# Graph network on one core: TensorE raises its semaphores once per group instead of once per product

## Chip, cores and metric

One core of one Trainium2 chip. The metric is the device time of one execution in microseconds. Three executions of the kernel before gave 2978.41, 2980.54 and 2985.08 us; their median is 2980.54 us.

## The reference, cut to what matters

3125 nodes of 256 features, 53125 edges (50000 both ways and 3125 self loops, sorted by dst). Four layers, each `x = layernorm(x + layer(x))`:

```python
def layer0(x):                      # applied twice with a relu between
    agg = segment_sum(x[src], dst) / maximum(count, 1)
    return agg @ Wl.T + bl + x @ Wr.T          # 256 -> 512 -> 256
def layer1(x):                      # three hops
    Hn = segment_sum(H[cols] * edge_weight, rows) @ Wn.T + bn
    H = elu(Hn + H @ Ws.T + bs)                # no elu after the last
def layer2(x):                      # interaction, out and in degrees in the scale
    msg = ((x @ W1)[src] + x[src] * x[dst] @ W2) / scale
    return normalize(leaky_relu(x @ W1 + segment_sum(msg, dst) + b))
def layer3(x):                      # attention, 8 heads of 32
    h = x @ W;  e = leaky_relu(a_src[src] + a_dst[dst])
    p = exp(e - segment_max(e, dst)[dst])
    out = segment_sum(h[src] * p, dst) / segment_sum(p, dst) + bias
    return layernorm(out)
```

Sums over edges in the first three layers are matrix products: a matrix of edge counts (or weights) between nodes is built once and multiplied with the node rows. The last layer gathers rows by edge and sums them with one-hot products.

## The kernel before, in words

A class `Program` holds one queue of instructions per engine. `op` (L125 and on) appends a function that first waits for its tokens (semaphore, count), then issues one instruction that raises that engine's own "done" semaphore by one, and returns the token of the new count. `T` (L315) is `op` for TensorE. Every engine runs its queue in order. Nodes are 25 tiles of 128 (`NODE_TILES`). Edges without self loops are 416 tiles of 128 (`EDGE_TILES`), four of which are a quad (`GROUP`).

**Stages in order of time.** About 40 to 300 us: the count matrix is built. VectorE makes windows of one-hots (L540), TensorE multiplies them (`build_pe`, L545 to L560), ACT (ScalarE) keeps finished windows (`build_act`, L562 to L581). TensorE and ACT load step numbers into registers and wait on semaphores against them.

332 to 530 us, first pass over the count matrix (`first_tile`, L1080), 530 to 739 us the dense layers (`to_hidden` L1197 and `from_hidden` L1212, products of four matmuls each, each matmul an `op`), 739 to 930 us the second pass (`multiply_tile`, L954 to L975). In a pass each of 24 further node tiles is the sum of 25 products in five groups of five. ACT widens the counts of a group from 16 to 32 bits into one buffer, `count_columns` (`widen_group`, L936): the cast of group g for the next tile waits until TensorE has used group g for this tile, which it learns from `s_a_used`, raised after each group. Beside these stages GpSimd scatters the edge weights into a dense matrix by indirect transfers (L794), paced by `multiplied_beside` (L827 to L838), which waits for given counts of TensorE's semaphores; VectorE forms the sums that go there (L849).

949 to 1990 us, three hops (`hops_pe`, L1457 and on; L1526 are the products with the dense weight matrix, which come from memory through a ring).

1990 to 2280 us, third pass and layer 2. 2280 to 2545 us, the expansion: 112 stages (`expansion_pe`, L2209 and on). In a stage VectorE builds one-hots (L2298), TensorE makes six products (`by_high`, L2226) that raise `s_first`, VectorE masks the result (`mask_rows`, L2311), and TensorE adds the masked rows up (`pick`, L2237), raising `s_picked`. Sixteen stages are a cut. GpSimd gathers rows by edge meanwhile (L2134), at the pace of the masks.

2565 to 2903 us, the merge: 440 steps in 110 quads. Rows of a quad lie in one of 16 places. For nine places of 16 they were gathered during the expansion, kept in memory, and are loaded by SyncE (`load_rows`, L2180); for seven of 16, so quads 96, 98, 100 and 102 at the end, GpSimd gathers them directly (L2134, four transfers each). Both wait in `place_free` (L2137) until the place is free: 4(quad - 16) + 28 steps done, so nine quads of steps before their own number. There are 104 quads of rows and, since a tile whose edges end at two node tiles takes two steps, 110 of steps. Between its quads GpSimd has one other piece, `gather_last` (L2453, 25 indirect transfers). VectorE scales the rows of quad q + 1 (`scale_rows`, L2486) and builds the one-hots of quad q (`node_hots`, L2492), which lie in two halves in turn, so that they wait for quad q - 2 to be multiplied. TensorE (`merge_pe`, L2531) loads 20 step registers at a time, waits for the one-hots once per quad, and adds each step's product to the bank of its node tile. A step is one instruction and shows as two matmul records. ACT (`merge_act`, L2536 and on) takes each node tile's sum when the step that ends it is done and starts that bank anew.

The semaphore of the merge is `s_mm`, raised once a step. Its readers are `place_free`, `node_hots` and `merge_act`:

```python
e.wait_ge(s_mm, mm0 + (quad - PLACES) * GROUP + GROUP - 1 + NODE_TILES)      # place_free
e.wait_ge(s_mm, quad * GROUP + (mm0 - GROUP))                                 # node_hots
e.wait_ge(s_mm, e.snap(ends_of_node[d], min_val=1, max_val=MERGE_STEPS + UNROLL))   # merge_act
```

The functions that the change touches, and what calls them:

## Time and profile before

| | us |
|---|---|
| median of the runs | 2980.54 (2978.41 to 2985.08) |
| span of the profiled execution | 2974.2 |
| TensorE busy | 2470.6 (83%) |
| VectorE busy | 1396.0 (47%) |
| ScalarE busy | 707.2 (24%) |
| GpSimd busy | 936.7 (31%) |
| mean granted TensorE clock | 0.920 |

The profiled execution has no device time of its own beside its span: the first to the last recorded instruction is 2974.2 us, and the median of the runs is 6.3 us above it.

How to read the table and the rows. PE is TensorE, PEld its weight loads, DVE VectorE, ACT ScalarE, POOL GpSimd, SP SyncE; L2531 is line 2531. A group of the page is: line, engine, operation, what it writes and reads, how often | busy us, mean ns of one | idle us of the engine just before it, and what ended most of that. A row of the timeline is: start, duration, engine, line, operation, how many in a row, and in brackets the idle time before with its releaser. "remote" and "another core or an unknown queue" stand for a semaphore event whose author the profile could not find, "issue" for time in which nothing shown was waited for. Matmuls are pipelined, so their single durations overlap.

### The profile page before, as it was taken

What the parts mean: (1) busy time and instruction counts of PE and PEld (TensorE: products, weight loads), DVE (VectorE), ACT (ScalarE), POOL (GpSimd) and SP (SyncE); (2) the same over time, 40 slices, a digit from 0 to 9 for tenths busy, and PEclk for the clock granted to TensorE, in tenths of its full rate; (3) what the DMA queues carried; (4) which work ended last, traced back from release to release, by engine and by line L of the source; (5) the groups of instructions that cost most, each with busy time, mean ns of one, the idle gap of its engine ahead of it and who ended that gap; (6) DMA issues with size and microseconds to landing.
All of it is one profiled execution on the core that took longest, in us unless ns stands there. A gap on an engine that the chain in (4) does not pass through costs nothing. (4 is left out here: it accounts for less than half of the span.)

```text
span 2974.2 us, 32381 instructions
## 1 busy us (share of the span) xinstructions
PE 2470.6 (83%) x9483; PEld 1621.2 (55%) x9484; DVE 1396.0 (47%) x3940; ACT 707.2 (24%) x1552; POOL 936.7 (31%) x927
## 2 busy tenths in 40 slices
PE   3677789897987999999999999999977886457680
PEld 2444788343766555565556555577743444345560
DVE  7999656455665001030101001455575664546668
ACT  3776545111443000010001000255400000103112
POOL 0000256666666000000000000012167666576740
PEclk9888999998998999999999999999988998678885
DMA  6565678343344743444444434333558887646641
GB/s 233 243 253 225 212 238 264 118 138 97 112 121 137 152 151 129 151 134 151 129 152 133 151 119 145 93 106 102 113 168 271 278 282 245 209 132 190 192 127 43
DMA packets 209534, 493.89 MB, mean 166 GB/s; under 512 B 46457, under 2 KB 128430, under 8 KB 209134
## 3 DMA queue, kind: packets, MB, share of 16 engines
q1 hardware_dynamic: 135185, 301.30, 32.2%
q10 hardware_dynamic: 38173, 133.27, 12.8%
q0 software_dynamic: 36032, 57.60, 7.1%
q8 instruction: 67, 1.10, 0.1%
q14 instruction: 77, 0.63, 0.1%
HBM read 374.71 MB, written 117.32 MB: 165 GB/s over the span
## 5 line engine op out<-in xcount | busy, mean ns | idle before, releaser
L794 POOL DMA_INDIRECT table_dense_weights<-pair_weight,dst x416 | 411.2, 988 | 563.5 <-DVE weights_c L849 324.8
L1526 PE MATMUL banks<-own_term,features_and_rows 128*128 128x391 f32 (+1 forms) x1656 | 552.3, 491 | 0.0
L2134 POOL DMA_INDIRECT features_and_rows<-table_heads,src x376 | 401.7, 1068 | 191.4 <-issue 107.9
L1526 PEld LDWEIGHTS banks<-own_term,features_and_rows 128*128 128x128 f32 x1656 | 312.2, 189 | 226.8
L1552 DVE TENSOR_SCALAR features_and_rows<-banks,hop_bias 128x391 f32<-128x391 f32 (+1 forms) x24 | 15.0, 625 | 762.2 <-PE banks L1526 762.2
L954 PE MATMUL banks<-split_rows,count_columns 128*128 128x512 f32 x1200 | 322.1, 415 | 19.6 <-issue 12.6
L2531 PE MATMUL banks<-features_and_rows,edge_to_window 128*128 x880 | 233.4, 427 | 104.5 <-DVE edge_to_window L2492 71.6
L1526 PE MATMUL banks<-features_and_rows 128*128 128x391 f32 (+1 forms) x840 | 282.4, 491 | 0.0
L954 PEld LDWEIGHTS banks<-split_rows,count_columns 128*128 128x128 f32 x1200 | 226.3, 193 | 76.8 <-issue 21.7
L2531 PEld LDWEIGHTS banks<-features_and_rows,edge_to_window 128*128 128x128 f32 x880 | 181.3, 210 | 156.5 <-issue 122.5
L558 PE MATMUL banks<-features_and_rows,pair_and_bias_rows 128*128 128x400 f16 x806 | 184.3, 388 | 87.1 <-DVE features_and_rows L540 51.9
L936 ACT CAST count_columns<-hidden 128x640 fp32r<-128x640 f16 x310 | 212.4, 723 | 157.2 <-PE banks L954 62.2
L1526 PEld LDWEIGHTS banks<-features_and_rows 128*128 128x128 f32 x840 | 158.4, 189 | 114.6
L2004 POOL DMA_INDIRECT ble_values_at_first_edge<-dst,row_of_first_edge x50 | 48.0, 961 | 516.9 <-DVE ln_rstd L1983 464.9
L1601 POOL DMA_INDIRECT features_and_rows<-table_hop,node_of_tail_row x6 | 5.7, 953 | 638.1 <-DMA table_hop<-tmp 637.1
L558 PEld LDWEIGHTS banks<-features_and_rows,pair_and_bias_rows 128*128 128x128 f16 x806 | 110.8, 152 | 160.9 <-issue 147.6
L540 DVE TENSOR_SCALAR features_and_rows<-counter_fp,features_and_rows 128x400 f16<-128x400 f16 x806 | 198.4, 335 | 0.0
L2226 PE MATMUL banks<-features_and_rows,pair_weight 128*104 128x512 bf16 (+1 forms) x672 | 169.8, 393 | 29.9 <-DVE features_and_rows L2298 19.1
L1543 ACT ACTIVATE features_and_rows<-banks,hop_bias 128x391 f32<-128x391 f32 (+1 forms) x24 | 14.1, 587 | 728.1 <-PE banks L1526 728.1
L1080 PE MATMUL banks<-split_rows,count_columns 128*128 128x258 f32 (+1 forms) x1200 | 158.6, 291 | 13.4 <-issue 10.2
L2237 PE MATMUL banks<-edge_to_window,edge_weight 104*128 104x512 f32 (+1 forms) x224 | 123.1, 634 | 53.2 <-DVE edge_to_window L2311 32.1
L2226 PEld LDWEIGHTS banks<-features_and_rows,pair_weight 128*104 128x104 bf16 x672 | 89.8, 137 | 131.9 <-issue 75.4
(425 smaller groups left out, 3016.8 us busy)
## 6 DMA issues: line engine op xcount, KB each, us to landing
hidden<-table_counts SPq DMA_DIRECT2D x305, 160.0 KB
table_dense_weights<-weights_c ACTq DMA_DIRECT2D x26, 1600.0 KB, 5.7
own_term<-table_dense_weights SPq DMA_DIRECT2D x52, 782.0 KB
features_and_rows<-table_rows_by_edge SPq DMA_DIRECT2D x58, 528.0 KB
own_term<-table_dense_weights SPq DMA_DIRECT2D x34, 780.5 KB
pair_and_bias_rows<-table_edge_rows ACTq DMA_DIRECT2D x50, 512.0 KB
weights_c<-table_edge_rows ACTq DMA_DIRECT2D x50, 512.0 KB
table_rows_by_edge<-features_and_rows SPq DMA_DIRECT2D x48, 528.0 KB
```

What stands on the lines that cost most here:

```text
L540: made = e.tensor_scalar(hot_ring[:, s % HOTS, q, :], counter[:, 0:WIDE], steps_key[:, q, s:s + 1], None, ALU.is_equal)
L558: m = e.matmul(banks[:, bass.ds(bank_at, WIDE)], low_ring[:, s // LOWS_AT_ONCE % LOW_BLOCKS, :, 2 * (s % LOWS_AT_ONCE) + q], hot_ring[:, s ...
L794: e.indirect_dma_start(out=self.table, out_offset=bass.IndirectOffsetOnAxis(ap=self.place[:, t:t + 1], axis=0), in_=self.values[:, t:t + 1 ...
L936: e.copy(in_group(count_columns, g), in_group(slot_of(q), g)).then_inc(s_a_wide, 1)
L954: m = e.matmul(to[:, 0:2 * DIM], lhs_of(k), both_pieces(k), start=(k == first), stop=False, skip_group_check=True)
L1080: m = e.matmul(to(wide), count_columns[:, k, :], piece(k, h, wide), start=(k == 0 and h == 0), stop=False, skip_group_check=True)
L1526: m = e.matmul(psum[b][:, 0:wide], z_block(block)[:, f * P:(f + 1) * P], streamed[tile % STREAM][:, lo - from_column:lo - from_column + wi ...
L2004: e.indirect_dma_start(out=t_start[c], out_offset=bass.IndirectOffsetOnAxis(ap=start_at[:, j:j + 1], axis=0), in_=node_pair[:, j, c * HEAD ...
L2134: e.indirect_dma_start(out=to[:, k, :], out_offset=None, in_=t_h, in_offset=bass.IndirectOffsetOnAxis(ap=src[:, t:t + 1], axis=0)).then_in ...
L2226: m = e.matmul(psum[i % 2][head_rows, 0:n], table[:, q, c, :], low_hot[i % 2][c][:, 0:n], start=(c == 0 and q == 0), stop=(c == 1 and q == ...
L2237: e.matmul(psum[2 + b % 2][:, 0:n], sum_heads[head_rows, at:at + P], masked[i % 2][head_rows, 0:n], start=(r == 0), stop=(r == SCAN_ROWS - ...
L2531: e.matmul(banks[:, bass.ds(column_at, ATT_ROW)], onehot[:, k % UNROLL, :], wide_rows[:, bass.ds(row_at, ATT_ROW)], start=False, stop=Fals ...
```

## The change

Where one product or one group of transposes takes several matmuls, only the last raises a semaphore (`last=`; the others are queued by `part`). `s_a_used` is raised after the third and the fifth group of a tile in the first two passes. `s_mm` is raised on the fourth step of a quad. `s_picked` is raised once per cut, and the wait for it in `mask_rows` is dropped. All waits are rewritten in the new counts. Waits against a register go through `wait_loaded`, which writes the loaded value ANDed with 511 into a second register and waits on that, in place of a register move. Instructions and their order are otherwise the same.

```diff
+        def part(self, e, fn, *waits):
...

+        def wait_loaded(e, sem, loaded, bound):
+            e.reg_alu(bound, loaded, 511, ALU.bitwise_and)
+            e.wait_ge(sem, bound)
-        T = lambda fn, *w: pr.op("pe", fn, *w)
+        T = lambda fn, *w, last=True: pr.op("pe", fn, *w) if last else pr.part("pe", fn, *w)
...
-                e.wait_ge(s_a_used, min(45 + 4 * (half_step - IN_ROWS) + 2 * half, of_group(Q1, 0) + NODE_TILES * COUNT_GROUPS - 1))
+                e.wait_ge(s_a_used, min(2 * (45 + 4 * (half_step - IN_ROWS) + 2 * half) // 5, used(Q2 - 1, COUNT_GROUPS - 1)))
-                e.wait_ge(pr.done["pe"], dense_layers_from[0] + max(1, 6 * (half_step - IN_LAYERS) - 10 + 3 * half))
+                e.wait_ge(pr.done["pe"], dense_layers_from[0] + max(1, (6 * (half_step - IN_LAYERS) - 10 + 3 * half) // 4))
...
+        USED_AT = (COUNT_GROUPS // 2, COUNT_GROUPS - 1)
+        used = lambda q, g: q * len(USED_AT) + (1 if g <= USED_AT[0] else 2) if q < Q3 else of_group(q - Q3, g) + Q3 * len(USED_AT)
-                    e.wait_ge(s_a_used, of_group(q - 1, g))
+                    e.wait_ge(s_a_used, used(q - 1, g))
-                    m.then_inc(s_a_used, 1)
+                    if g in USED_AT:
+                        m.then_inc(s_a_used, 1)
...
                     m = T(lambda e, q=q, l=l, r=r, ps=ps, wdt=wdt: e.matmul(ps[:, 0:wdt], l, r, start=(q == 0), stop=(q == 3)),
-                          freed if q == 0 else None, scaled[c], xt_ready if q == 0 else None, l_w)
+                          freed if q == 0 else None, scaled[c], xt_ready if q == 0 else None, l_w, last=q == len(pairs) - 1)
-                          freed if mt == 0 else None, made[c])
+                          freed if mt == 0 else None, made[c], last=mt == K_HID - 1)
...
-        V(lambda e: e.tensor_scalar(merge_control[0:1, MERGE_STEPS:], ends_at, float(UNROLL), None, ALU.add), (s_merge, 1))
+        ends_known = V(lambda e: e.tensor_scalar(merge_control[0:1, MERGE_STEPS:], ends_at, float(UNROLL * GROUP + GROUP - 1), None, ALU.add), (s_merge, 1))
+        V(lambda e: e.tensor_scalar(merge_control[0:1, MERGE_STEPS:], merge_control[0:1, MERGE_STEPS:], 2, None, ALU.arith_shift_right),
+          ends_known)
...
-                e.wait_ge(s_mm, mm0 + (quad - PLACES) * GROUP + GROUP - 1 + NODE_TILES)
+                e.wait_ge(s_mm, mm0 + (quad - PLACES) + (GROUP - 1 + NODE_TILES) // GROUP)
...
-                e.matmul(psum[2 + b % 2][:, 0:n], ...).then_inc(s_picked, 1)
+                m = e.matmul(psum[2 + b % 2][:, 0:n], ...)
+                if r == SCAN_ROWS - 1:
+                    m.then_inc(s_picked, 1)
...
-                if i >= 2:
-                    e.wait_ge(s_picked, i - 1)
...
-                e.wait_ge(s_picked, SCAN_ROWS * (b + 1))
+                e.wait_ge(s_picked, b + 1)
...
-                e.wait_ge(s_mm, quad * GROUP + (mm0 - GROUP))
+                e.wait_ge(s_mm, quad + (mm0 - 1))
...
-                    e.wait_ge(s_begun, step % 32)
-                    e.matmul(banks[:, bass.ds(column_at, ATT_ROW)], onehot[:, k % UNROLL, :], wide_rows[:, bass.ds(row_at, ATT_ROW)],
-                             start=False, stop=False, skip_group_check=True).then_inc(s_mm, 1)
+                    e.wait_ge(s_begun, step & 31)
+                    m = e.matmul(banks[:, bass.ds(column_at, ATT_ROW)], onehot[:, k % UNROLL, :], wide_rows[:, bass.ds(row_at, ATT_ROW)],
+                                 start=False, stop=False, skip_group_check=True)
+                    if k % GROUP == GROUP - 1:
+                        m.then_inc(s_mm, 1)
...
-                e.wait_ge(s_mm, e.snap(ends_of_node[d], min_val=1, max_val=MERGE_STEPS + UNROLL))
+                wait_loaded(e, s_mm, ends_of_node[d], bound)
```

The groups of transposes, the running sum over nodes, the two build functions and the wait of the weight stream are changed in the same two ways.

## Rows read from the trace of the kernel before

**Rows 1.** The page's groups (columns: "How to read the table" above).

```profile
L1526 PE MATMUL banks<-own_term,features_and_rows 128*128 128x391 f32 (+1 forms) x1656 | 552.3, 491 | 0.0
...
L2531 PE MATMUL banks<-features_and_rows,edge_to_window 128*128 x880 | 233.4, 427 | 104.5 <-DVE edge_to_window L2492 71.6
...
L936 ACT CAST count_columns<-hidden 128x640 fp32r<-128x640 f16 x310 | 212.4, 723 | 157.2 <-PE banks L954 62.2
...
L540 DVE TENSOR_SCALAR features_and_rows<-counter_fp,features_and_rows 128x400 f16<-128x400 f16 x806 | 198.4, 335 | 0.0
```

**Rows 2.** Busy table by stretch: each engine's busy us (instructions), PEclk, DMA share, GB/s.

```profile
739.00:930.00 191.00, 166.89 (x675) 129.70 (x675) 133.75 (x175) 84.73 (x131) 126.61 (x132) 0.94 0.39 112
2290.00:2545.00 255.00, 190.95 (x692) 102.16 (x692) 144.84 (x283) 1.49 (x2) 165.64 (x168) 0.87 0.81 263
2640.00:2902.00 262.00, 197.88 (x784) 155.83 (x783) 169.95 (x191) 53.63 (x225) 162.89 (x148) 0.90 0.56 174
```

**Rows 3.** Chain of waits in 2540:2974, shares by line.

```profile
by line: PE banks L2531 37.1%; another core or an unknown queue 14.3%; issue 13.6%; DVE features_and_rows L2486 8.1%; DVE edge_to_window L2492 4.1%; DVE ln_stats L759 3.9%; DVE features_and_rows L2409 2.3%; DVE features_and_rows L2592 2.3%;
```

**Rows 4.** Timeline 2584:2642 of TensorE, VectorE, GpSimd (start, us, work, idle before).

```profile
2587.35 3.39 PE L2531 MATMUL banks<-features_and_rows,edge_to_window 128*128 x8 [4.26 <-DVE edge_to_window L2492]
2597.20 3.88 PE L2531 MATMUL banks<-features_and_rows,edge_to_window 128*128 x8 [6.46 <-DVE edge_to_window L2492]
...
2610.23 0.69 DVE L2492 TENSOR_TENSOR edge_to_window<-banks,dst_of_step 128x512 f32<-128x512 f32 x1 [12.20 <-issue]
...
2628.43 0.69 DVE L2492 TENSOR_TENSOR edge_to_window<-banks,dst_of_step 128x512 f32<-128x512 f32 x1 [16.35 <-remote]
...
2611.63 0.94 POOL L2453 DMA_INDIRECT tmp<-table_running_max,row_of_last_edge  x1 [0.30 <-issue]
```

**Rows 5.** Timeline 2716:2742 (TensorE, VectorE), and VectorE's wait in 2640:2902.

```profile
2715.73 2.39 PE L2531 MATMUL banks<-features_and_rows,edge_to_window 128*128 x10
...
2728.86 0.69 DVE L2492 TENSOR_TENSOR edge_to_window<-banks,dst_of_step 128x512 f32<-128x512 f32 x1 [7.36 <-remote]
...
DVE edge_to_window L2492 <- remote: 43.9, 7, 7.4
```

**Rows 6.** Timeline of TensorE, 2840:2852.

```profile
2840.45 9.16 PE L2531 MATMUL banks<-features_and_rows,edge_to_window 128*128 x40 [0.65 <-issue]
2850.67 1.59 PE L2531 MATMUL banks<-features_and_rows,edge_to_window 128*128 x6 [1.07 <-DVE edge_to_window L2492]
```

**Rows 7.** GpSimd: wait and group in 2540:2905, last transfer; TensorE's end.

```profile
POOL features_and_rows L2134 <- remote: 7.6, 4, 3.4
...
L2134 POOL DMA_INDIRECT features_and_rows<-table_heads,src x184 | 203.9, 1108 | 98.9 <-issue 47.2 <-PE banks L2531 28.9 <-DMA table_running_max<-features_and_rows 9.2
...
2871.97 0.95 POOL L2134 DMA_INDIRECT features_and_rows<-table_heads,src  x1 [0.30 <-issue]
...
2875.72 17.55 PE L2531 MATMUL banks<-features_and_rows,edge_to_window 128*128 x64 [6.46 <-DVE edge_to_window L2492]
2893.82 9.16 PE L2531 MATMUL banks<-features_and_rows,edge_to_window 128*128 x40 [0.55 <-issue]
```

**Rows 8.** Waits in the expansion, 2290:2545 (us in total, times, longest).

```profile
PE banks L2237 <- DVE edge_to_window L2311: 31.7, 10, 9.4
...
DVE edge_to_window L2311 <- remote: 30.1, 6, 6.3
```

**Rows 9.** Waits in 530:739 (first row) and 739:930.

```profile
PE banks L1197 <- issue: 15.2, 13, 2.5
...
ACT count_columns L936 <- PE banks L954: 55.6, 31, 5.7
...
PE banks L954 <- ACT count_columns L936: 6.9, 5, 2.7
```

**Rows 10.** Timeline of TensorE, 504:512.

```profile
507.85 0.28 PE L1080 MATMUL banks<-split_rows,count_columns 128*128 128x256 f32 x1 [0.43 <-issue]
```

**Rows 11.** Timeline of TensorE in the hops.

```profile
999.70 21.24 PE L1526 MATMUL banks<-own_term,features_and_rows 128*128 128x391 f32 x64
```

More of the change, by code:

```diff
@@ L142, in op, with emit @@
         return sem, self.count[sem.name]
+    def part(self, e, fn, *waits):
+        waits = [w for w in waits if w is not None]
+        def emit(eng):
+            for s, v in waits:
+                eng.wait_ge(s, v)
+            fn(eng)
+        self.queue[e].append(emit)
     def dma(self, e, sem, out, in_, *waits):
@@ L565, in build_act @@
             regs = [e.alloc_register(f"window_end_{k}") for k in range(ROTATING)]
+            bound = e.alloc_register("window_end_step")
             for b in [RUN_BANK, RUN_BANK + 1, *range(ROTATING)]:
@@ L639, in residual_gnn @@
                 m = T(lambda e, i=i, values=values, lo=lo, n=n: e.transpose(psum[i][0:n, lo:lo + P], values[:, lo:lo + n], ident[:, :]),
-                      keyed, c_id, counts_kept)
+                      keyed, c_id, counts_kept, last=lo == lasts[-1][0])
             at_row = turned_rows[:, r * 512:(r + 1) * 512]
@@ L733, in late_prep @@
                     m = T(lambda e, i=i, values=values, lo=lo, n=n: e.transpose(psum[i][0:n, lo:lo + P], values[:, lo:lo + n],
-                                                                                ident[:, :]), prepared["halves"], found)
+                                                                                ident[:, :]), prepared["halves"], found,
+                          last=lo == lasts[-1][0])
                 A(lambda e, i=i, r=r: e.copy(index_row[:, r, 0:3 * P], psum[i][:, 0:3 * P]), m)
@@ L1009, in run @@
                 m = multiply_rows(e, psum[0], lambda k: count_columns[:, k, :], (k,), 0, True)
-                if k % COUNT_GROUP == COUNT_GROUP - 1:
+                if k % COUNT_GROUP == COUNT_GROUP - 1 and k // COUNT_GROUP in USED_AT:
                     m.then_inc(s_a_used, 1)
@@ L1035, in residual_gnn @@
                 next(steps)
-        multiplied_tail = (s_a_used, of_group(Q1, COUNT_GROUPS - 1))
+        multiplied_tail = (s_a_used, used(Q1, COUNT_GROUPS - 1))
         tail_split = split(K_FOLD, psum[0][:, 0:DIM], multiplied_tail)
@@ L1081, in first_tile @@
                                      skip_group_check=True)
-                m.then_inc(s_a_used, 1)
+                if g in USED_AT:
+                    m.then_inc(s_a_used, 1)
             first_folded(e, n, to, False)
@@ L1167, in running_sum @@
             before = lambda n: ps[:, n * 32:n * 32 + NODE_TILES]
-            T(lambda e: e.matmul(before(0), triangle, counts, start=True, stop=True), freed, tri)
+            T(lambda e: e.matmul(before(0), triangle, counts, start=True, stop=True), freed, tri, last=False)
             m = T(lambda e: e.matmul(before(1), ones[:, :], counts, start=True, stop=True))
@@ L1268, in residual_gnn @@
         widen(Q2 + 1)
-        split(K_FOLD, psum[0][:, 0:DIM], (s_a_used, of_group(Q2, COUNT_GROUPS - 1)))
+        split(K_FOLD, psum[0][:, 0:DIM], (s_a_used, used(Q2, COUNT_GROUPS - 1)))
         folded2 = [build_fold(1, s_row2)]
@@ L1299, in turn0 @@
                     m = T(lambda e, ps=ps, j=j, k=k: e.transpose(ps[:, k * P:(k + 1) * P], x[:, j, k * P:(k + 1) * P], ident[:, :]),
-                          freed, t)
+                          freed, t, last=k == K_IN - 1)
                 reader[i] = A(lambda e, ps=ps, j=j: e.copy(xT[:, :, j * P:(j + 1) * P],
@@ L1628, in hops_sp @@
                         e.load([reg], steps_needed[0:1, tile:tile + 1])
-                        e.wait_ge(weights.steps, e.snap(reg, min_val=1, max_val=STEPS))
+                        wait_loaded(e, weights.steps, reg, stream_register[1])
                     elif tile == BODY * 4:
@@ L1762, in residual_gnn @@
                 m = T(lambda e, ps=ps, j=j, k=k: e.transpose(ps[:, k * P:(k + 1) * P], xT[:, k, j * P:(j + 1) * P], ident[:, :]),
-                      freed, *hops_done)
+                      freed, *hops_done, last=k == K_IN - 1)
             turned_late[j] = i, ps, m
@@ L1816, in residual_gnn @@
         widen(Q3 + 1)
-        tail_ready3 = split(K_FOLD, psum[0][:, 0:DIM], (s_a_used, of_group(Q3, COUNT_GROUPS - 1)))
+        tail_ready3 = split(K_FOLD, psum[0][:, 0:DIM], (s_a_used, used(Q3, COUNT_GROUPS - 1)))
         low_value = src_lo_hot[:, :, :].rearrange("p k n -> p (k n)").rearrange("p (c n) -> p c n", c=2)
@@ L2061, in first_rows @@
             e.wait_ge(*prepared["index"])
-            e.wait_ge(s_a_used, of_group(Q3 + NODE_TILES - 1, COUNT_GROUPS - 1))
+            e.wait_ge(s_a_used, used(Q3 + NODE_TILES - 1, COUNT_GROUPS - 1))
             for k in range(ROWS_KEPT // 2):
@@ L2236, in pick @@
                 at = P - HEADS - r * HEADS
-                e.matmul(psum[2 + b % 2][:, 0:n], sum_heads[head_rows, at:at + P], masked[i % 2][head_rows, 0:n],
-                         start=(r == 0), stop=(r == SCAN_ROWS - 1)).then_inc(s_picked, 1)
+                m = e.matmul(psum[2 + b % 2][:, 0:n], sum_heads[head_rows, at:at + P], masked[i % 2][head_rows, 0:n],
+                             start=(r == 0), stop=(r == SCAN_ROWS - 1))
+                if r == SCAN_ROWS - 1:
+                    m.then_inc(s_picked, 1)
             def turn_held(b):
@@ L2397, in residual_gnn @@
         T(lambda e: e.matmul(psum[6][:, 0:P], back[:, 0:1].broadcast_to([P, P]), ident[:, :], start=True, stop=True),
-          spread_max, masks_ok)
+          spread_max, masks_ok, last=False)
         m = T(lambda e: e.matmul(psum[6][:, P:2 * P], back[:, last:].broadcast_to([P, P]), ident[:, :], start=True, stop=True))
```

19 lines of the change are left out of this document (10 added, 9 removed).

## The prediction

> **What bounds the kernel now.** I first took the granted clock and the busy table by stretch, then the chain that ended last, then the timeline of the places where that chain is not TensorE. No single engine bounds the whole run. In the hops TensorE does: its largest group shows idle 0.0 before 1656 matmuls [rows 1]. In the build VectorE does, with idle 0.0 before its 806 comparisons [rows 1]. The merge is different. In 2640 to 2902 us TensorE is busy 197.9 of 262 us, VectorE 170.0, GpSimd 162.9 [rows 2]: nobody is full. The group of its matmuls (L2531) shows 104.5 us idle, 71.6 of them before a release by VectorE's one-hots (L2492) [rows 1]. And the chain of the last 434 us is TensorE's matmuls for only 37.1%, while 14.3% is "another core or an unknown queue" and 13.6% "issue" [rows 3]. There is one core, so an unknown releaser is a semaphore event that the profile could not pair with work in time.
>
> The timeline says what it is. The one-hots of a quad (four steps, two matmul records each) may be built once the quad two before is multiplied. TensorE multiplied one quad from 2587.35 on for 3.39 us, so until 2590.74, and the next from 2597.20 to 2601.08 [rows 4]. The one-hots that need the first of them start at 2610.23, 19.5 us after it ended, VectorE having sat idle 12.20 us; those that need the second start at 2628.43, 27.4 us after, with 16.35 us idle [rows 4]. GpSimd meanwhile issues one indirect transfer after another, 0.94 us long and 0.30 apart [rows 4]. It recurs later: the quad until 2718.12 is answered at 2728.86, VectorE idle 7.36 us [rows 5]. In a calm place the same loop makes 40 matmuls, five quads, in 9.16 us [rows 6]. So in such spells TensorE has multiplied, and its count reaches VectorE 10 to 27 us late. I read it so: every step raises the semaphore by one, VectorE needs the fourth raise of a quad, and while GpSimd issues transfers the raises are delivered slowly, one behind the other: 14 to 18 us between one-hots are 3.5 to 4.5 us a raise, 9.2 us at 2720 are 2.3. The number of raises is what the change divides by four. In 2640 to 2902 alone VectorE idles 43.9 us before L2492 on the unknown releaser [rows 5].
>
> **Part 1, the merge.** 440 raises become 110, and every condition stands at the same step as before, since both sides counted in quads already; only the node sums' ends are rounded up, by at most three steps, 3 x 2 x 0.229 = 1.4 us [rows 6]. ACT waits there for a sum of a bank reused several tiles later, so I cost it at nothing; if that cover is gone it is 1.4 us at the last tile. One tiny VectorE operation is added in the hops, where TensorE shows no idle: 0.
>
> What goes, if the delay goes: of the chain's 434 us, 62 us unknown and 59 us issue [rows 3]. Issue contains the loads of step registers, 22 of them, 10.22 us from block start to block start less 9.16 [rows 6], so 1.07 us x 22 = 23 us, which stay. Up to about 98 us are then at stake. But GpSimd is late next. Its queue is nearly continuous: in 2540 to 2905 it idles only 28.9 us for TensorE and 7.6 us for unknown releasers beside its fixed 0.30 us per transfer [rows 7]. Its last transfer starts at 2871.97 [rows 7]. With those 36.5 us gone it starts at 2835.5. It belongs to quad 102 of 110; eight quads remain, at the 64 matmuls in 17.55 us of the end [rows 7], plus one transfer and one scaling (0.95 + 1.25) and some landing, say 3 us: 2835.5 + 3 + 17.5 = 2856. TensorE's last block ends at 2893.82 + 9.16 = 2903.0 [rows 7]. The gain with GpSimd as the floor is 47 us. I take **42**, since one raise per quad can still be late: at 2.3 to 4.5 us each it can exceed the 2.04 us (10.22 / 5) that a quad takes. Bounds: 3 (a raise costs only its own time, below) and 76 (the 184 transfers average 1.108 us against an undisturbed 0.95, so 29 us more could go [rows 7]).
>
> **Part 2, the expansion.** 112 raises of `s_picked` become 7, and the mask's wait on it goes; TensorE's order implied it. There VectorE's masks (L2311) idle 30.1 us on unknown releasers and TensorE's picks (L2237) wait 31.7 us for masks [rows 8], while GpSimd is busy 165.6 of 255 us with 168 instructions [rows 2], 216 us with 0.30 each. `s_first`, the raise that the mask really needs, stays at one per stage, so the raises are halved only. Of 31.7 us I take a quarter: **8**; ends 0 and 31.
>
> **Part 3, the dense layers and transposes.** Groups of four now raise once; ACT and VectorE always waited for the last. TensorE idles 15.2 us on issue at L1197 between 530 and 739 [rows 9]. I take a third: **5**; ends 0 and 15. Thresholds of the scatters in GpSimd's queue are rounded down, so they go up to three matmuls earlier; they are paced, not late: 0.
>
> **Part 4, the casts.** `s_a_used` goes from five raises a tile to two in the first two passes. ACT's cast of group 0 was released by group 0's products and is now released by group 2's. Second pass: 166.9 us of matmuls on 24 tiles of five groups are 1.4 us a group [rows 2]; the release comes 2.8 us later, three casts of 0.72 us follow [rows 1], and TensorE needs group 0 again after groups 3 and 4, 2.8 us later. Cast 0 has 2.1 us to spare, cast 3 at the next boundary 3 x 1.4 - 0.7 = 3.5. ACT idles 55.6 us for TensorE there, so it has the room; TensorE waits for casts only 6.9 us [rows 9]. Fewer raises make those fewer, a late one now holds three casts. Sum: **3** gained, ends -15 and +15 (48 tiles x 0.6 us would be +29).
>
> **Part 5, replaced register instructions.** A move becomes an AND one for one, in the build, the stream loads and the merge: 0. In the build the cover is VectorE's full 198.4 us group [rows 1].
>
> **Sum.** 42 + 8 + 5 + 3 = 58. Against the profiled execution's span, 2974.2 - 58 = 2916.2. The median of the runs, 2980.54, lies 6.3 above that span, which I keep: **2922 us**.
>
> **What speaks against it.** At 507.85 a single matmul of a group (L1080), which raises nothing itself, comes after 0.43 us of issue, and so do its neighbours [rows 10]. So TensorE itself can stall in such a spell with no raise attached. That is either the backlog of earlier raises, or a disturbance that counts time and not raises.
>
> **Rivals.**
> A. *The raise is cheap, or the spell is a matter of time.* The hops run 64 matmuls of 391 columns, no raise, in 21.24 us, 0.85 ns a column [rows 11]; the merge's 264 columns would be 224 ns against 229 [rows 6], so 10 ns a raise, 330 x 0.010 = 3 us. If GpSimd's activity delays whatever comes, one raise per quad waits as long as the fourth did, and the time is 2972 to 2983: no change or barely faster. The Trainium skill (TensorE: Matmul & The Clock Gate, "The cost: per-tile semaphore tail") has raises serialize at 26.3 ns each; by that an estimate for the 330 of the merge is 8.7 us, 2972. The trace disagrees in size at the spells: three extra raises would be 0.08 us there, against 19.5 and 27.4 us of lateness. Chance 0.17.
> B. *GpSimd's floor is soft.* Its stretched transfers come from the same congestion and the other stages give their upper halves: 76 + 15 + 8 + 5 = 104, so 2876. Chance 0.17.
> C. *Slower.* The casts' coarser release decides. The place is ACT's queue in passes one and two: where a raise of group 2 comes over 2.1 us late, cast 0 is not ready and TensorE stands. For it: waits of up to 5.7 us for TensorE before casts [rows 9]. At 0.6 us on each of 48 tiles it is 29 us; with A's merge the time is about 3005, and with the merge's gain it is only a smaller gain. Point: mean added lateness of the last-needed cast over 0.1 us a tile with nothing gained elsewhere. Chance 0.09.
> D. *Forecast*, gains of 35 to 80 us: 0.57.
> Since both sides read the same counts, the change does nothing only as in A.
>
> **Numbers.** What a measurement of this kernel tells from no change is about 0.2%, 6 us. Faster by more: D, B and a little of A, 0.77. Same: 0.14. Slower: 0.09. The range takes in B's end, 2866, and A's, 2984, leaving C and larger gains out.
>
> **What would show it.** Right: before L2492 the 43.9 us of unknown idle in the merge's last 262 us fall under 15, GpSimd's wait for L2531 (28.9) shrinks to a few, the stretch from the exponentials to the last merge matmul is 40 us shorter, the hops are unchanged within 1 us. Wrong: one-hots still start 4 us or more after the quad's last matmul (A), TensorE L954 and L1080 idle behind L936 grows past 20 us (C), transfers average 0.95 (B).

## The result, and the profile after

The change made the kernel slower by a little: 3009.92 us median of five executions (2988.39 to 3014.08) against 2980.54 (2978.41 to 2985.08, also of five), ratio 1.0083 with a 95% interval of 1.0049 to 1.0117. Ten later executions of the changed kernel on another chip, beside thirty-one of the kernel before, gave 2983.32 against 2975.31 us, ratio 1.0020 (0.9998 to 1.0041): by these alone it may also be no change. The forecast was 2922 us. The traced execution of the changed kernel is its fastest one, 2988.39 us with a span of 2986.6, 12.4 us over the span of before. So the trace can show where some 12 us went, and not where the median's 29 did.

The page after, its groups (line, work, count | busy us, mean ns | idle before, releaser):

```profile
L1548 PE MATMUL banks<-own_term,features_and_rows 128*128 128x391 f32 (+1 forms) x1656 | 552.3, 491 | 0.0
...
L974 PE MATMUL banks<-split_rows,count_columns 128*128 128x512 f32 x1200 | 315.9, 410 | 21.6 <-ACT count_columns L956 11.0
```

L1548 answers to L1526 of [rows 1]: the hops did not change. Where the time went, I read from the starts of each stage's first product in both traces: the first pass's last product is 8.0 us later than before, the dense layers' last 13.7, the hops start 14.4 later, the merge's first product is 18.3 later and its last 12.4. So some 14 us were lost before the hops, some 4 more up to the merge, and the merge gave back 6, not 42.

VectorE's waits in 2540 to 2925 of the changed kernel (us in total, times, longest):

```profile
DVE edge_to_window L2516 <- remote: 87.6, 18, 19.1
DVE edge_to_window L2516 <- PE banks L2555: 36.1, 27, 3.9
DVE edge_to_window L2516 <- issue: 10.4, 7, 5.3
```

With one raise per quad the waits before the one-hots are 134 us; they were 142 with four. The unknown releaser, which [rows 5] showed with 43.9 us in the merge's last 262, was to fall under 15; it has 51.3 us in the same last stretch, 2652 to 2914 here. GpSimd's waits for TensorE and unknown releasers in the merge are 32.1 us, against 36.5 [rows 7]. The timeline of the changed kernel around the 25 transfers of `gather_last` (VectorE, TensorE, GpSimd) answers to [rows 4]:

```profile
2605.98 0.69 DVE L2516 TENSOR_TENSOR edge_to_window<-banks,dst_of_step 128x512 f32<-128x512 f32 x1 [5.30 <-issue]
2624.96 0.69 DVE L2516 TENSOR_TENSOR edge_to_window<-banks,dst_of_step 128x512 f32<-128x512 f32 x1 [17.13 <-remote]
...
2645.99 0.69 DVE L2516 TENSOR_TENSOR edge_to_window<-banks,dst_of_step 128x512 f32<-128x512 f32 x1 [19.12 <-remote]
...
2606.99 3.88 PE L2555 MATMUL banks<-features_and_rows,edge_to_window 128*128 x8 [4.38 <-DVE edge_to_window L2516]
2625.97 3.88 PE L2555 MATMUL banks<-features_and_rows,edge_to_window 128*128 x8 [15.10 <-DVE edge_to_window L2516]
...
2609.31 0.95 POOL L2477 DMA_INDIRECT tmp<-table_running_max,row_of_last_edge  x1 [0.30 <-issue]
2610.57 0.95 POOL L2477 DMA_INDIRECT tmp<-table_running_max,row_of_last_edge  x1 [0.30 <-issue]
```

The same spell, with waits of 17 and 19 us, though one raise stands in place of four. The run e1 below has every raise back; its two one-hots in the same place:

```profile
2619.98 0.69 DVE L2515 TENSOR_TENSOR edge_to_window<-banks,dst_of_step 128x512 f32<-128x512 f32 x1 [16.43 <-remote]
2640.30 0.69 DVE L2515 TENSOR_TENSOR edge_to_window<-banks,dst_of_step 128x512 f32<-128x512 f32 x1 [18.47 <-remote]
```

From the end of a quad's last product to the start of the one-hots that need it are 8.1, 22.3 and 35.1 us for three quads in turn with one raise each, and 10.5, 22.8 and 33.7 us with four. The lateness does not come from the number of raises.

### The profile page after: what moved, and what is told of

Read it like the earlier page. It is cut to its first block, busy times and chain, and to the rows that moved or that the text cites. A ratio compares the mean times of both kernels' runs of the same rounds, so it can differ in the third digit from the quotient of the medians.

```text
span 2986.6 us, 32707 instructions
## 1 busy us (share of the span) xinstructions
PE 2474.8 (83%) x9483; PEld 1622.1 (54%) x9484; DVE 1395.3 (47%) x3941; ACT 704.6 (24%) x1552; POOL 942.0 (32%) x927
## 3 DMA queue, kind: packets, MB, share of 16 engines
q10 hardware_dynamic: 38173, 133.27, 12.9%
## 4 chain that ended last, share of the span: by engine, by line
PE 61%; DVE 18%; another core or an unknown queue 8%; issue 7%; ACT 2%; DMA 2%; ACTq 0%; DVEq 0%; SPq 0%
PE banks L1548 27%; PE banks L974 7%; DVE features_and_rows L556 5%; PE banks L2555 5%; PE banks L2250 4%; PE banks L1101 3%; PE banks L1518 2%; PE banks L2261 2%; PE banks L1535 2%; DVE pair_and_bias_rows L553 2%; PE banks L1219 2%; PE banks L1234 2%; DVE features_and_rows L2510 1%; PE banks L1936 1%
## 5 line engine op out<-in xcount | busy, mean ns | idle before, releaser
L1548 PE MATMUL banks<-own_term,features_and_rows 128*128 128x391 f32 (+1 forms) x1656 | 552.3, 491 | 0.0
L2158 POOL DMA_INDIRECT features_and_rows<-table_heads,src x376 | 407.7, 1084 | 178.9 <-issue 110.2
L1548 PEld LDWEIGHTS banks<-own_term,features_and_rows 128*128 128x128 f32 x1656 | 312.2, 189 | 226.8
L974 PE MATMUL banks<-split_rows,count_columns 128*128 128x512 f32 x1200 | 315.9, 410 | 21.6 <-ACT count_columns L956 11.0
L1548 PE MATMUL banks<-features_and_rows 128*128 128x391 f32 (+1 forms) x840 | 282.4, 491 | 0.0
L974 PEld LDWEIGHTS banks<-split_rows,count_columns 128*128 128x128 f32 x1200 | 223.9, 191 | 75.7 <-issue 23.9
L574 PE MATMUL banks<-features_and_rows,pair_and_bias_rows 128*128 128x400 f16 x806 | 186.2, 398 | 84.1 <-DVE features_and_rows L556 37.3
L1548 PEld LDWEIGHTS banks<-features_and_rows 128*128 128x128 f32 x840 | 158.4, 189 | 114.6
L1101 PE MATMUL banks<-split_rows,count_columns 128*128 128x258 f32 (+1 forms) x1200 | 162.4, 293 | 20.2 <-issue 15.0
L1101 PEld LDWEIGHTS banks<-split_rows,count_columns 128*128 128x128 f32 x1200 | 153.6, 198 | 25.7 <-issue 24.1
```

The lines of the kernel that those rows point to most:

```text
L574: m = e.matmul(banks[:, bass.ds(bank_at, WIDE)], low_ring[:, s // LOWS_AT_ONCE % LOW_BLOCKS, :, 2 * (s % LOWS_AT_ONCE) + q], hot_ring[:, s ...
L974: m = e.matmul(to[:, 0:2 * DIM], lhs_of(k), both_pieces(k), start=(k == first), stop=False, skip_group_check=True)
L1101: m = e.matmul(to(wide), count_columns[:, k, :], piece(k, h, wide), start=(k == 0 and h == 0), stop=False, skip_group_check=True)
L1548: m = e.matmul(psum[b][:, 0:wide], z_block(block)[:, f * P:(f + 1) * P], streamed[tile % STREAM][:, lo - from_column:lo - from_column + wi ...
L2158: e.indirect_dma_start(out=to[:, k, :], out_offset=None, in_=t_h, in_offset=bass.IndirectOffsetOnAxis(ap=src[:, t:t + 1], axis=0)).then_in ...
```

## The experiments

Stages below are from the first to the last product of the stage's line in the run's trace. There is one trace a kernel, and stages scatter between kernels that do not differ in them: the dense layers by up to 7 us, the first pass by 13, the merge by 11; so I compare groups of traces. Runs e1 to e4, e5 to e8 and e9 to e12 were on three different chips, and each time is compared with the kernel before on the same chip. The traced executions of e6 and e7 are the slowest of their ten, some 15 us over the medians, which may make their stages long.

**Which part costs.** `e1_all_raises` keeps the register ANDs and puts every raise back, `e2_merge_only` raises once per quad in the merge alone, `e3_all_but_merge` undoes the merge, `e4_casts_undone` the casts. The core of e1's edit:

```diff
-        T = lambda fn, *w, last=True: pr.op("pe", fn, *w) if last else pr.part("pe", fn, *w)
+        T = lambda fn, *w, last=True: pr.op("pe", fn, *w)
-        USED_AT = (COUNT_GROUPS // 2, COUNT_GROUPS - 1)
+        USED_AT = tuple(range(COUNT_GROUPS))
-                    if k % GROUP == GROUP - 1:
-                        m.then_inc(s_mm, 1)
+                    m.then_inc(s_mm, 1)
```

with the counts in the waits of before; e2, e3 and e4 are subsets of it.

> The changed kernel with every raise of the kernel before put back (per matmul, per step, per group) and the old counts in the waits; only the register ANDs stay. Theory S (the slower time comes from fewer or later raises): 2978 to 2985 us, as the kernel before. Rival R (it comes from the AND that replaces the register move, or from the shifted code): 3000 to 3015 us.

Measured: 2991.11 us against 2990.31 for the kernel before beside it, ratio 1.0001 (0.9983 to 1.0020). The absolute numbers of the expectation missed by 6 us, because the kernel before was 10 us slower here than on the first chip; against it, theory S holds and R falls: the AND costs nothing that this interval of about 6 us could tell.

> Only the merge raises once per quad. Theory of my forecast (a spell costs per raise): 2935 to 2945 us, merge 40 us shorter. Rival (a spell holds whatever raise comes): within 6 us of e1, with VectorE's L2515 one-hots still idle over 80 us in the merge.

Measured: 2994.35 us, ratio 1.0031 (1.0008 to 1.0055), so it gains nothing, and 3.2 us over e1. Its merge took 328.0 us against 332.5 in e1 and 334.1 before, and VectorE idled 80.7 us before the one-hots on the unknown releaser and 51.0 on TensorE. The rival holds.

> The merge raises once per step again, all else as in the changed kernel. If the loss sits in the first pass, the dense layers and the second pass, where the trace after is 14 us later at the first hop: 2995 to 3015 us and the first hop's first product 10 us or more later than in e1. If the loss was a matter of the merge: as e1.

Measured: 2998.20 us, ratio 1.0019 (0.9996 to 1.0041). The hops' first product came at 964.2 us, 12 later than e1's 952.0 and as late as the changed kernel's 963.7. The loss lies ahead of the hops.

> The changed kernel with the five raises a tile for the casts, and the scatters' thresholds in them, put back. If the coarser release of the casts costs (my rival C): 10 to 25 us faster than the changed kernel, and TensorE's first pass ends 5 us or more earlier. If the products' groups cost: as the changed kernel, 3005 to 3015 us.

Measured: 2995.27 us, ratio 1.0020 (0.9996 to 1.0044). The first pass took 189.3 us, 7 less than the 196.8 of the changed kernel, but the dense layers kept their 212.0. The time fits neither expectation: 2995.27 is under the 3005 to 3015 of the one, and by the 8 us that the changed kernel costs in e5 the gain is some 3 us, not 10 to 25.

**The same reference, and each loss by itself.**

```diff
# e6_casts_only: e1, and
+        USED_AT = (COUNT_GROUPS // 2, COUNT_GROUPS - 1)
# e7_groups_only: e1, and
+        T = lambda fn, *w, last=True: pr.op("pe", fn, *w) if last else pr.part("pe", fn, *w)
```

Each also keeps the changed kernel's conditions for GpSimd's scatters where they count these raises: e6 those of the two passes, up to two groups of products earlier than before, e7 those of the dense layers, up to three products earlier. So neither separates the raises from the earlier scatters.

> The changed kernel again, unchanged, for a reference on the same chip as the others. If the parts add up (merge -6, casts +9, dense groups +7, read from five profiles): 6 to 12 us over the kernel before. If the first result's 29 us were real: 20 us or more over it.

Measured: 8.0 us over the kernel before (2983.32 to 2975.31), as the parts said, though the interval (0.9998 to 1.0041) still holds no change; the 29 us of the first result did not come back, and what made them is not known.

> All raises of before, except that the casts' semaphore is raised twice a tile. Theory C (the coarser release costs in the first pass): its products take 196 to 200 us from first to last against 186 to 191 without, and 5 to 10 us over e1 in time; the second pass unchanged. Rival (only together with the grouped products): within 3 us of e1.

Measured: 2980.28 us, ratio 1.0007 (0.9984 to 1.0029). First pass 193.7 us, 2 under the range named, second pass 179.9. In the passes and layers together, from the first product of the first pass to the first transpose of the hops, it took 608.1 us against 600.5 of e1. The time shows no difference that its interval can tell, so it decides between neither expectation.

> All raises of before, except that transposes and dense products raise once per group, with the scatters' thresholds in those counts. Theory (thresholds rounded down let GpSimd run denser, and TensorE's raises come later): dense layers 209 to 213 us from first to last product against 202 to 205 with all raises, 5 to 9 us over e1 in time. Rival (noise): 202 to 206 us.

Measured: 2981.25 us, ratio 1.0023 (1.0005 to 1.0041), 5.9 us over the kernel before beside it. Dense layers 212.2 us against 201.4 to 205.5 with all raises. Over all traces of e1 to e12 and the two kernels the four without grouped products took 202.1 (before), 205.5 (e1), 203.3 (e2) and 201.4 (e6), and the ten with them 205.1 to 212.2, mean 209.8: 6.7 us more. For the coarser casts the first pass is 188.8 to 201.9 us, mean 194.5, in nine traces, and 186.2 to 191.2, mean 189.2, in the five without: 5.3 us more. The parts add up: 6.7 + 5.3, less 1.6 in the second pass and 2.8 in the merge, is 7.6 us, beside the 8.0 of e5.

**What the spell is.**

```diff
# e8_spaced_last: behind each transfer of gather_last
+                if j:
+                    e.wait_ge(s_filler, j)
+                e.iota(filler[:, :], [[1, 64]], base=0, channel_multiplier=0).then_inc(s_filler, 1)
# e12_spaced_wide: eight of these behind each transfer
# e9_no_last
-            for j in range(NODE_TILES):
-                e.indirect_dma_start(out=mx[:, j, :], ...).then_inc(s_last, 16)
+            e.tensor_copy(mx, own_score).then_inc(s_last, 16 * NODE_TILES)
```

> The changed kernel with a small GpSimd operation of about 0.2 us, and the wait for it, between the 25 indirect transfers of L2477. Theory (raises of TensorE are held while GpSimd issues transfers back to back): the two waits of 17 and 19 us before the one-hots between 2605 and 2646 shrink under 6 us each, and the sixteenth quad is multiplied 15 us or more earlier, counted from the merge's first. Rival (the holding comes from the transfers' traffic or from TensorE itself): the waits stay over 12 us each.

Measured: 2988.50 us, ratio 1.0034 (1.0011 to 1.0057). It tested little: the small operation fell into the 0.30 us between two transfers, and the transfers came every 1.31 us instead of every 1.25. The waits were 9.40, 17.78 and 8.02 us, where the changed kernel on the same chip (e5) had 8.0, 18.4 and 12.9; neither expectation came true.

> The changed kernel without the 25 indirect transfers of L2477 (the gathered maxima are replaced by a copy of the nodes' own scores). Theory (GpSimd's transfers hold TensorE's raises): the waits of 17 and 19 us before the one-hots near 2620 and 2640 are gone, no wait over 8 us in the first ten quads, and the merge is 31 us shorter by the transfers or more. Rival (the spell belongs to TensorE or to the merge's start): waits of 12 us and more stay within the first ten quads.

e9 leaves out the gather of the segment maxima, which weigh each node's own row.

> The changed kernel with eight small GpSimd operations between the 25 transfers of L2477, so that one starts every 3 us or so instead of every 1.25. Theory (the holding depends on the share of time that GpSimd issues transfers): waits before the one-hots shrink under 4 us each during these transfers, though they last 75 us. Rival (any transfer holds TensorE as long as such transfers go on): waits of 10 us and more throughout those 75 us.

Measured, one execution each, beside one of 2991.14 us for the kernel before: e9 2965.83, e12 3041.91. VectorE's waits in the fifty microseconds where the changed kernel had its two long ones, in e9 (2586 to 2636), and then in e12 during the transfers (2615 to 2695), with GpSimd's timeline there:

```profile
DVE edge_to_window L2514 <- PE banks L2553: 7.6, 5, 3.4
...
DVE edge_to_window L2514 <- remote: 3.5, 3, 1.9
```

```profile
DVE edge_to_window L2522 <- PE banks L2561: 1.2, 2, 1.1
```

```profile
2618.85 0.95 POOL L2479 DMA_INDIRECT tmp<-table_running_max,row_of_last_edge  x1 [0.16 <-issue]
2619.81 1.94 POOL L2484 IOTA filler<- 128x64 int32 x8
2621.91 0.94 POOL L2479 DMA_INDIRECT tmp<-table_running_max,row_of_last_edge  x1 [0.16 <-issue]
```

Without the transfers the spell is gone; with them every 3.06 us it is gone too, in one trace each. So this spell takes GpSimd's indirect transfers, and takes them dense. Both also say what the merge is bound by: without 31 us of transfers it took 300.3 us against 327 to 338, and with 45 us more of GpSimd it took 377.7. GpSimd's queue sets its length, and this one spell is slack in it. The later ones are not, as e18 shows below.

**A burst where TensorE is full.** In the hops TensorE never idles and raises once per block; GpSimd has two transfers there.

```diff
# e10_burst: in hops_pool, behind the two transfers of hop 0
+                if hop == 0:
+                    for k in range(40):
+                        e.indirect_dma_start(out=burst[:, k, :], out_offset=None, in_=burst_from,
+                                             in_offset=bass.IndirectOffsetOnAxis(ap=src[:, k:k + 1], axis=0)).then_inc(s_burst, 16)
# e11_burst_raises: e10, and in hops_pe, first phase
+                            elif p == 0 and b != held_banks[-1]:
+                                m.then_inc(s_extra, 1)
```

> The changed kernel with 40 indirect transfers more on GpSimd (32 bytes a row, into an own tile) right after its two of hop 0, in a place where TensorE raises only once per block and nothing else of GpSimd runs. Theory (transfers hold TensorE's completions whatever they raise): in the 50 us of the burst TensorE's products of hop 0 come with gaps, the hops 10 us or more longer. Rival (only queued raises suffer): TensorE's pitch stays 329 ns there and the hops are within 3 us.

> As e10, with every product of the first phase of hop 0 raising a semaphore that nobody waits for. If raises are what suffers in a spell: TensorE has gaps in the burst, and the hops are 20 us or more longer than in e10. If the number of raises does not matter: as e10 within 3 us.

Measured: e10 3048.11 us, hops 999.7 us from first to last product against 969.0 in the changed kernel (963.9 to 970.8 in all twelve traces of e1 to e9, e12 and the two kernels); e11 3032.20 us, hops 1001.2. One execution each. TensorE's timeline in e10, and GpSimd's first and last transfer of the burst:

```profile
1029.31 21.24 PE L1548 MATMUL banks<-own_term,features_and_rows 128*128 128x391 f32 x64
1050.39 4.44 PE L1548 MATMUL banks<-features_and_rows 128*128 128x391 f32 x13
1055.52 0.49 PE L1548 MATMUL banks<-features_and_rows 128*128 128x391 f32 x1 [0.70 <-issue]
1056.94 0.49 PE L1548 MATMUL banks<-features_and_rows 128*128 128x391 f32 x1 [0.93 <-issue]
1059.75 0.81 PE L1548 MATMUL banks<-features_and_rows 128*128 128x391 f32 x1 [2.32 <-issue]
1062.54 0.81 PE L1548 MATMUL banks<-features_and_rows 128*128 128x391 f32 x1 [1.98 <-issue]
...
1081.49 0.81 PE L1548 MATMUL banks<-features_and_rows 128*128 128x391 f32 x1 [1.99 <-issue]
1084.29 5.58 PE L1548 MATMUL banks<-features_and_rows 128*128 128x391 f32 x8 [1.99 <-issue]
```

```profile
1031.12 0.94 POOL L1632 DMA_INDIRECT burst<-w_t,src  x1 [0.30 <-issue]
...
1079.82 0.94 POOL L1632 DMA_INDIRECT burst<-w_t,src  x1 [0.30 <-issue]
```

TensorE keeps its pace for the first 24 us of the burst, then takes one product every 2.8 us in place of one every 0.33, and is free again some 4 us after the last transfer. (Two other transfers stand directly before the burst, from 1028.58 on.) The busy table of e10 during the burst's start, in its hold and after it (busy us and count of TensorE, of its loads, VectorE, ScalarE, GpSimd, granted clock, DMA share, GB/s):

```profile
1020.00:1050.00 30.00, 30.00 (x92) 17.22 (x91) 0.00 (x0) 0.00 (x0) 16.24 (x18) 1.00 0.67 143
1055.00:1085.00 30.00, 8.98 (x13) 2.97 (x12) 0.00 (x0) 0.00 (x0) 19.67 (x21) 0.56 0.14 30
1090.00:1120.00 30.00, 30.00 (x93) 17.22 (x91) 0.00 (x0) 0.00 (x0) 0.00 (x0) 1.00 0.60 207
```

The granted clock was 1.00 before and after and 0.56 in the hold, where a product took 0.81 us instead of 0.49; the first two products behind a gap still took 0.49, so the gaps came first and the lower clock after them. The products in the hold raise nothing, apart from one a block, and nothing that the profile shows is waited for. In e11 the hold begins 23.7 us after its first transfer and has the same steps, so the 175 extra raises do not make it: the hops of the two are 1.5 us apart. Nor does a raise cost TensorE's pace here. The 64 products before the hold, each of which raises a semaphore in e11, take as long as in e10:

```profile
1011.52 21.24 PE L1550 MATMUL banks<-own_term,features_and_rows 128*128 128x391 f32 x64
```

The Trainium skill (TensorE: Matmul & The Clock Gate, "The cost: per-tile semaphore tail") has 26.3 ns a raise, measured on small tiles that run side by side; by that an estimate for the 56 extra raises among these 64 products is 1.5 us. The trace does not agree: 21.24 us in both.

**Rate or number, raises or thresholds: not settled.**

```diff
# e13_burst_pauses and e16: 42 transfers in three bursts of 14, GpSimd paused between
# e14_burst_pitch and e17: 40 transfers, five small operations behind each
# e15_groups_later and e18: e7, and
-    max(1, (6 * (half_step - IN_LAYERS) - 10 + 3 * half) // 4)
+    max(1, (6 * (half_step - IN_LAYERS) - 10 + 3 * half + 7) // 4)
```

> The burst beside the hops again, but as three bursts of 14 transfers (17.5 us) with a pause of some 6 us of GpSimd after each. In e10 and e11 TensorE stalled only from the 24th us of the burst on. If something has to fill up first and drains in a pause: no stall at all, TensorE's pitch 329 ns throughout, hops 965 to 971 us. If the stall counts transfers however they are spread: it begins about the 20th transfer, with 10 us or more of gaps.

> The burst of 40 with five small GpSimd operations after each transfer, so one transfer every 2.3 us or so. If the rate decides: no stall. If the transfers' number decides: a stall from the 20th transfer on, 46 us after the first.

> As e7 (dense products and transposes raise once per group), but with the scatters' thresholds in the dense layers up to two groups of products later instead of rounded down. If rounding down, which lets GpSimd scatter earlier and denser, costs the 8 us of the dense layers: 201 to 206 us from first to last product there. If the fewer raises themselves cost: 209 to 213 us as in e7.

These three ran on another chip than e1 to e12, and there the kernel before itself took 2804.34 us (2801.02 to 2810.74). e13 took 2800.28 and e14 2800.23, one execution each; e15 took 2804.10 (ratio 0.9996, 0.9986 to 1.0006). The same three once more:

> e13 again, since in e13's executions no kernel showed a stall, the kernel before included (2804 us). Where the dense layers of this very execution take over 200 us (so that the stalls are there): if something fills up and drains in a pause, the hops take 965 to 971 us and TensorE has no gaps in the bursts of 14. If transfers are only counted, gaps from the 20th transfer on, hops over 975 us.

> e14 again for the same reason: 40 transfers at one every 2 us or slower. If the rate decides: hops 965 to 971 us and no gap. If their number decides: gaps from the 20th transfer on.

> e15 again, where stalls are there. If the rounded-down thresholds of the scatters cost the dense layers' 8 us: 201 to 206 us from first to last product. If the fewer raises themselves cost: 209 to 213 us, as in e7, e4, e3 and the changed kernel.

A further chip, and again 2800.84 us for the kernel before, with 2803.30 for e16, 2798.87 for e17 and 2799.78 for e18 (ratio of e18 0.9998, 0.9988 to 1.0007). The hops took 959 to 961 us in all six, four of them with their bursts, and neither pauses nor pitch can be judged, since no trace there shows the hold. What they show is the kernel without it. TensorE's waits in e18 over the first pass, the dense layers and most of the second pass (330 to 800 us), the three largest and the one on issue, and then its busy table over the same work (TensorE, loads, VectorE, ScalarE, GpSimd, clock, DMA share, GB/s):

```profile
PE banks L750 <- DVE node_of_tail_row L747: 6.6, 1, 6.6
PE banks L1101 <- ACT count_columns L956: 5.9, 4, 2.5
PE banks L1118 <- ACT features_and_rows L1141: 3.8, 2, 3.2
...
PE banks L1101 <- issue: 0.2, 1, 0.2
```

```profile
332.00:800.00 468.00, 447.77 (x2240) 329.46 (x2240) 315.89 (x1124) 193.25 (x329) 327.09 (x331) 0.99 0.60 187
```

Only 0.2 us of "issue" stand in front of TensorE's products, also when the second pass is taken to its end, where the changed kernel had 47 us of it in both passes and the dense layers (15.0 at L1101, 11.2 at L1234, 10.6 at L974, 9.8 at L1219). Against the kernel before's trace, the passes and layers took 514.5 us in e18 instead of 600.0, the expansion 268.7 instead of 345.4, the merge 298.8 instead of 334.1, the hops 959.2 instead of 966.9. Part of the expansion's gain comes back: from its last product to the merge's first are 68.7 us instead of 35.0. Where GpSimd issues few transfers or none, the chips agree: 333.4 against 332.1 us up to the first pass, 270.4 against 271.9 for the third pass and layer 2, 71.5 against 71.6 behind the merge. GpSimd's transfers in the merge were no shorter, 1106 ns on average against 1108 [rows 7]; what fell is its waiting for TensorE:

```profile
POOL features_and_rows L2156 <- PE banks L2554: 5.5, 18, 0.3
```

Those are 5.5 us where the kernel before had 28.9, and 7.6 more on unknown releasers [rows 7]. By these numbers the hold costs the merge some 35 us, and keeps GpSimd waiting for 31 of them. But these are different chips and slightly different kernels, and no trace of the kernel before exists on a chip without the hold, so it is likely, and not shown, that the hold makes the whole difference.

No version was faster than the kernel before on its chip clear of noise, of those that leave nothing out.

## Why the prediction was wrong

**The step that failed** is the reading of the late counts: "every step raises the semaphore by one, VectorE needs the fourth raise of a quad, and while GpSimd issues transfers the raises are delivered slowly, one behind the other". The runs showed in its place that a quad is as late with one raise as with four: 22.3 and 35.1 us (changed kernel) against 22.8 and 33.7 (e1), and the merge gained 2.8 us, not 42. And they showed that products which raise nothing are held too: in the hops one came every 2.8 us, whether each raised something (e11) or not (e10). That it is the same hold in the merge is argued, not shown. For it: a quad has eight product records, 8 x 2.8 = 22 us, and the changed kernel's one-hots in the spell come 18.98 and 21.03 us apart (2605.98, 2624.96, 2645.99). By that my 3.5 to 4.5 us "a raise" were two products. Against it: the merge's eight products begin within 3.88 us there, so what is late by the profile comes behind their start.

**The evidence was in the rows I had.** [Rows 10] showed a product without a raise behind 0.43 us of nothing but "issue", and its neighbours alike. (The eight products of [rows 4] in 3.88 us, where 40 take 9.16 [rows 6], are no such sign: the granted clock was 0.50 there and 1.00 here.) I named [rows 10] against myself and gave the rival built on it, A, 0.17. It had the merge right: 326.9 to 338.3 us with one raise per quad, mean 332.0 in six traces (e8, e9 and e12 change the merge itself and are left out), against 332.5 to 337.2, mean 334.8 in five with four; 2.8 us, within the scatter, where A said 3 and the sum said 42. That the 2.8 meets A's 3 is luck, since e11 shows no cost of a raise in TensorE's pace. And A's time, 2972 to 2983 us, was missed too (3009.92): A put nothing on the losses ahead of the hops. My own sign of being wrong, one-hots 4 us or more behind the quad's last product, came with 8 to 35 us.

**GpSimd as the floor** was right: e9 and e12 move the merge one for one with GpSimd's work. The size of the term was near as well: where the hold is gone (e13 to e18) GpSimd waits 31 us less and the merge takes 298.3 to 301.2 us, 33 to 36 less than before, against the 42 of the sum. What failed is that fewer raises would take the hold away. The expansion's 8 us did not come either: 345.4 to 353.2 us with the old raises and the wait, in five traces, 345.3 to 357.5 without, in nine.

**The dense layers' 5 us** had the wrong sign: 6.7 us lost. The step costed the rounded-down thresholds at 0, "they go up to three matmuls earlier; they are paced, not late". Whether they are the cause or the later raises are, stays open; e15 and e18 were meant for it and ran where there is no hold. There the kernel with grouped products takes as long as the kernel before (0.9996 and 0.9998), whichever thresholds it has: the dense layers take 173.6 and 173.8 us with the later ones, 173.6 to 174.3 with the rounded-down ones (e13, e14, e16, e17). That more of GpSimd's transfers fall into the dense layers' time, or closer together, is not borne out: they are 139 or 140 in the four traces without grouped products and 140 to 143 in the ten with them, whose stage is longer by as much.

**The casts' 3 us** had the wrong sign too: 5.3 us lost in the first pass, with -1.6 in the second. That is rival C's place, at 0.2 us a tile against the 0.6 I wrote; its 3005 us assumed that this was the whole. C's mechanism is not shown. TensorE's waits for casts in both passes are 8.6 to 21.6 us, mean 16, with the coarser release (nine traces), and 8.9 to 18.2, mean 14, without (five), so they carry some 2 us; C's own sign, over 20 us, came in two traces of nine. In the first pass of the changed kernel the waits on "issue" grew more, from 10.2 to 15.0 us (L1080, now L1101). The looser conditions of the scatters in the passes, which the prediction left out, are the untested rival: 104 or 105 of GpSimd's transfers fall into the first pass with them, 103 or 104 without.

**The register ANDs** at 0 were right as far as e1 can tell, and so were the hops, 969.0 against 966.9 us within a scatter of 7.

## What to carry to other kernels

When a consumer starts long after its producer's last record, look first whether instructions of the producer that raise nothing are late in the same places; if they are, fewer signals may not help. Put the granted clock beside the durations before calling a product slow. A count of raises is not a cost by itself here: 330 fewer gave about 3 us, within the scatter. And where GpSimd issues indirect transfers back to back beside a busy TensorE, price the stretch by a trace of that very stretch on more than one chip, and take looser conditions for GpSimd there as a risk: whether they cost anything stayed open here.

## What the runs showed of the hardware that I had not expected

Dense indirect transfers by GpSimd, one every 1.25 us, held TensorE in the hops to one product every 2.8 us, from 24 us after the first of the burst until 4 us after the last (e10, e11); at one every 3.06 us they did not hold it in the merge (e12). VectorE's one-hots kept their 0.69 us in a spell and GpSimd's transfers their 0.95. And it is not so on every chip: where e1 to e12 ran, the kernel before took 2975 to 2991 us, and where e13 to e18 ran 2801 to 2804, 6% less, with GpSimd's transfers at the same pace and no hold. I have no explanation of either, and what in GpSimd's transfers holds TensorE was not found. One rival is untested: every execution here has the profiler's span beside its time, so no run tells whether the recording of instructions takes part in the hold.
